# The last image's first two quarters: GpSimd additions against accumulating DMAs

## Chip, cores and metric

One core of a Trainium2 chip runs the whole program. The metric is the device time of one execution in microseconds. A time is given as the median of several runs; beside it stands one profiled execution, whose rows are quoted.

## The reference, cut to what matters

```python
# x: (16, 128, 64, 64) float32, NCHW
x = x + L0(gn(x))     # 3x3 convolution with three weight planes, each quantised, clipped and summed
x = x + L1(gn(x))     # attention-free layer on 128 channels, below
# gn: group norm, 32 groups of 4 channels

def L1(x):            # xf = x as (b, 128, 4096)
    q, k, v = Wq @ xf, Wk @ xf, Wv @ xf           # 64 x 4096 each
    ek = exp(k)
    num, den = exp(B) @ (ek * v), exp(B) @ ek
    return Wm @ (q * (num / den))                 # 128 x 4096
```

The change concerns the last "+": the sum of L1's output and its input x (the residual) for the last image.

## The kernel before

The channels lie on the 128 partitions. An image is 4096 pixels and goes in four quarters k = 0 to 3 of PX = 1024 columns (512 KB of float32 each). Four buffers `xr[0..3]` form a ring of images: an image is loaded into one, the first layer's result is added in place, then the second layer's result is added in place, and the quarters are stored from it. The phases are a software pipeline: while image p is in the first layer's convolution, p-1 and p-2 are in the second layer. The order of the work is written out by hand in slots of a phase, separately for each engine; semaphores tie the engines together.

In a normal image, a quarter of the second layer ends so: TensorE multiplies by Wm into PSUM (`mix`, L684), ScalarE copies the result from PSUM to the buffer `y2[k % 2]` (a part of `shared`) in `evict` (L964), GpSimd issues a DMA from `y2` onto `xr` with an addition on the way (`add_mix`, L1695), and its landing is counted by the semaphore `y_added[k % 2]`. SP waits for it (L438) and issues the store to DRAM (`store`, L440). GpSimd's own arithmetic in the body is the low halves of the split operands and the small statistics.

The last image runs behind the last convolution, with nothing beside it, in the order of the table LAST_ORDER (keys and values, sums, queries, mix, each with its quarter). Its four quarters end in two ways:

- Quarters 2 and 3: VectorE adds straight from PSUM to `xr` (`second_residual`, L1456) and raises `second_done`.
- Quarters 0 and 1: ScalarE copies from PSUM to `y2[k]` (`last_evict`, L973, raising `last_evicted`), and GpSimd adds `y2[k]` to `xr` in two halves of 512 columns (`last_add`, L1676 to L1681, raising `last_added` once per half). It is the last work in GpSimd's program.

SP stores the last image's quarters in the order 0, 1, 2, 3. Before each one it waits for that quarter's addition: `last_added` at 2 and 4, then `second_done` at 1 and 2 (L436). As a queue works in order, a wait for quarter 1 also holds back quarters 2 and 3. At the very end SP waits for all stores to land (L494). `y_added` counts 32 per image on each of its two semaphores, since each landing adds 16.

Of the kernel before, what the change touches and what calls it, by code (L numbers as in the profile page):

```python
# [20 lines left out]
ALU = mybir.AluOpType  # L21
# [6 lines left out]
B, H, W = 16, 64, 64  # L28
# [6 lines left out]
PX = ROWS * W  # L35
HALF = PX // 2
# [73 lines left out]
def conv_layers_kernel(nc, x, g_pos, g_neg, bias, in_factor, out_factor, Wq, Wk, Wv, Bm, Wm, out):  # L110
# [6 lines left out]
    with ctx:  # L117
        def sb(name, shape, dt=F32):
            return ctx.enter_context(nc.sbuf_tensor(name, shape, dt))

        def sem(name):
            return ctx.enter_context(nc.semaphore(name))
# [3 lines left out]
        xr = [sb(f"xr{i}", [P, H * W]) for i in range(RING)]  # L126
# [7 lines left out]
        y2 = [shared[:, k * PX:(k + 1) * PX] for k in range(2)]  # L134
# [217 lines left out]
        y_added = [sem("y_added0"), sem("y_added1")]  # L352
        second_done = sem("second_done")
        last_evicted = sem("last_evicted")
        last_added = sem("last_added")

        def waits_apart(eng, *waits):

            values = [v if isinstance(v, int) else eng.to_reg(v) for _, v in waits]
            eng.wait_ge(consts_made, 1)
            for (s, _), v in zip(waits, values):
                eng.wait_ge(s, v)
# [27 lines left out]
        def nth(image, per_image, m, back=0):  # L392

            return image * per_image + (m + 1 - back * per_image)
# [22 lines left out]
        def phases(eng, phase):  # L417

            phase(0, 0, (False, False, True, True))
            phase(1, 1, (False, True, True, True))  # L420
            for p in range(2, B - 1):
                phase(p, p % RING, (True, True, True, True))
            phase(B - 1, (B - 1) % RING, (True, True, True, False))
            phase(B, B % RING, (True, True, False, False))

        @block.sync
        def _(sp):
            def load(image, m, g):
                cols = slice(g * PX, (g + 1) * PX)
                sp.dma_start(xr[m][:, cols].rearrange("p (a n) -> p a n", a=1),  # L430
                             x_v[:, bass.ds(image, 1), cols]).then_inc(loaded[g], 16)

            def store(image, m, k):

                if isinstance(image, int) and image == B - 1:
                    sp.wait_ge(*((last_added, 2 * k + 2) if k < 2 else (second_done, k - 1)))  # L436
                else:
                    sp.wait_ge(y_added[k % 2], nth(image, 32, 16 * (k // 2) + 15))  # L438
                cols = slice(k * PX, (k + 1) * PX)
                sp.dma_start(out_v[:, bass.ds(image, 1), cols],  # L440
                             xr[m][:, cols].rearrange("p (a n) -> p a n", a=1)
                             ).then_inc(stored[k], 16)

            for g in range(NG):
                load(0, 0, g)
            for t, src in ((gp, gp_v), (gn, gn_v)):
                sp.dma_start(t[:, 0:CK], src[:, 0, :]).then_inc(g_loaded[0], 16)
            sp.dma_start(inf[:, :], in_factor.partition_broadcast(P)).then_inc(factors_loaded, 16)
            for i in range(1, NP):
                sp.dma_start(gp[:, i * CK:(i + 1) * CK], gp_v[:, i, :]).then_inc(g_loaded[i], 16)  # L450
                sp.dma_start(gn[:, i * CK:(i + 1) * CK], gn_v[:, i, :]).then_inc(g_loaded[i], 16)
            sp.dma_start(bcol[:, :], bias.rearrange("(c a) -> c a", a=1)).then_inc(others_loaded, 16)
            sp.dma_start(outf[:, :], out_factor.partition_broadcast(P)).then_inc(others_loaded, 16)
            sp.dma_start(wqk_in[0:IC, :], Wq).then_inc(small_loaded, 16)
            sp.dma_start(wqk_in[IC:P, :], Wk).then_inc(small_loaded, 16)
            sp.dma_start(wv_in[0:IC, :], Wv).then_inc(small_loaded, 16)
            sp.wait_ge(zeroed, 1)
            sp.dma_start(bm_in[0:IC, 0:IC], Bm).then_inc(small_loaded, 16)
            sp.dma_start(bm_in[IC:P, IC:P], Bm).then_inc(small_loaded, 16)
            sp.dma_start(wm_in[:, 0:IC], Wm).then_inc(small_loaded, 16)  # L460
            sp.dma_start(wm_in[:, IC:P], Wm).then_inc(small_loaded, 16)
            sp.wait_ge(head_stats, NG)
            for g in range(NG):
                sp.wait_ge(stats_in[0], g + 1)
                load(1, 1, g)

            def phase(p, m, images):
                prev2, prev, cur, nxt = images
                if prev2:
                    for k in range(1, NG):  # L470
                        store(p - 2, (m + 2) % RING, k)
                if isinstance(p, int) and p == 0:

                    sp.wait_ge(w_turned, 9)
                    sp.wait_ge(sums_made, 2 * NP)
                if isinstance(p, int) and p == 1:
                    for i in range(NP):
                        sp.wait_ge(w_diff[i], 1)
                    sp.wait_ge(small_turned, 1)
                if nxt and not (isinstance(p, int) and p + 2 >= B):  # L480
                    for g in range(NG):
                        sp.wait_ge(stats_in[0], nth(p + 1, NG, g))
                        if prev2:
                            sp.wait_ge(stored[g], nth(p, 16, 15, 2))
                        load(p + 2, (m + 2) % RING, g)
                if prev and cur:
                    store(p - 1, (m + 3) % RING, 0)
                if not cur:
                    for k in range(NG):
                        store(p - 1, (m + 3) % RING, k)  # L490

            phases(sp, phase)
            for k in range(NG):
                sp.wait_ge(stored[k], 16 * B)  # L494
# [1091 lines left out]
        def _(pool):  # L1586
# [88 lines left out]

            def last_add(m, k):  # L1676

                for h in range(2):
                    waits_apart(pool, (last_evicted, k + 1))
                    xh = xr[m][:, k * PX + h * HALF:k * PX + (h + 1) * HALF]  # L1680
                    nc.gpsimd.tensor_tensor(xh, xh, y2[k][:, h * HALF:(h + 1) * HALF], ALU.add  # L1681
                                            ).then_inc(last_added, 1)

            def rows_low(image, parity, g):
                for k, pair in enumerate(PAIRS):
# [21 lines left out]
            def phase(p, m, images):  # L1707
                prev2, prev, cur, nxt = images
                before, two_before = (m + 3) % RING, (m + 2) % RING
                spread_at, moments_at, low_at = ((EACH if prev else FIRST)[name]  # L1710
                                                 for name in ("X_SPREAD", "X_MOMENTS", "LOW"))
                for slot in range(SLOTS):
                    second_layer(p, m, slot, images)
                    if nxt and slot == spread_at:
                        spread_stats(0, p + 1)
                    if prev and slot == X1_SPREAD:
                        spread_stats(1, p - 1)
                    if cur and slot in low_at[2:]:
                        rows_low(p, m % 2, low_at.index(slot))
                    if nxt and slot in low_at[:2]:  # L1720
                        rows_low(p + 1, 1 - m % 2, low_at.index(slot))
                    if nxt and slot == moments_at:
                        scale_x(p + 1)
                    if prev and slot == X1_MOMENTS:
                        scale_z(p - 1)
                if not cur:
                    add_mix(p - 2, two_before, 3)
                    last_rest(p - 1, 2, duo_flat[:, 0:PX])
                    last_rest(p - 1, 3, z32)
                    for k in range(2):  # L1730
                        last_add(before, k)
# [31 lines left out]
```

## Time and profile before

| | us |
|---|---|
| median of 3 runs | 1474.59 (1474.12 to 1475.69) |
| profiled execution, own time | 1475.87 |
| its span | 1473.8 |
| mean granted TensorE clock | 0.992 |
| TensorE busy | 1430.0 (97%) |
| VectorE busy | 1346.0 (91%) |
| ScalarE busy | 1194.6 (81%) |
| GpSimd busy | 555.5 (38%) |

The span goes from the first instruction of the program to the last; some 2 us of the execution lie around it. Engines in rows: PE is TensorE (PEld its weight loads), DVE is VectorE, ACT ScalarE, POOL GpSimd, SP SyncE; a q behind a name is that engine's queue, which issues DMAs. L440 is line 440 of the kernel. A row's tiles are written "out<-in", with buffer numbers left out, so that `xr<-shared` is any of the transfers from `y2` onto an image. A DMA's "us to landing" runs from the start of its issue until its semaphore has its full count.

### The profile page before, as it was taken

Reading aid. Unit: us, or ns where it says so; the run is one execution under the profiler, and the core shown is the slowest. Engines: PE = TensorE matmul, PEld = TensorE weight load, DVE = VectorE, ACT = ScalarE, POOL = GpSimd, SP = SyncE. Lnnn points to the kernel's source line nnn. Section 1 sums busy time; section 2 is a strip of 40 time slices with the busy share of each in tenths; the row PEclk is TensorE's granted clock in tenths of the full one; section 3 lists DMA queues with packets and bytes.
Section 4 is the critical chain, followed back from the end, with each engine's and each line's share of the span. In section 5 each row is a group of like instructions: output and inputs, shape, how many; then the busy total and the mean of one; then the engine's idle time right before and its main releaser. Section 6 shows DMA issues by size and latency. Waiting matters only on the chain. (4 is left out here: it accounts for less than half of the span.)

```text
span 1473.8 us, 24096 instructions
## 1 busy us (share of the span) xinstructions
PE 1430.0 (97%) x8632; PEld 664.1 (45%) x8632; DVE 1346.0 (91%) x2018; ACT 1194.6 (81%) x1569; POOL 555.5 (38%) x687
## 2 busy tenths in 40 slices
PE   3999999999999999999999999999999999999996
PEld 3644444444444444444444444444444444444442
DVE  7699898999999999998999999899999989999887
ACT  6658798887988888888887989788898888976674
POOL 2212335343433624334352433535244253433323
PEclk9999999999999999999999999999999999999998
DMA  5011012223222222412322231232322222222133
GB/s 216 7 52 58 1 30 58 90 56 114 58 53 91 58 87 58 115 44 57 101 58 86 58 115 33 55 101 58 101 58 71 73 58 86 58 58 58 30 79 122
DMA packets 29174, 103.85 MB, mean 70 GB/s; under 512 B 4032, under 2 KB 4224, under 8 KB 29056
## 3 DMA queue, kind: packets, MB, share of 16 engines
q1 hardware_dynamic: 20416, 70.86, 13.1%
q0 software_dynamic: 8640, 31.46, 11.3%
q8 instruction: 69, 1.13, 0.3%
q14 instruction: 49, 0.40, 0.1%
HBM read 37.29 MB, written 33.55 MB: 48 GB/s over the span
## 5 line engine op out<-in xcount | busy, mean ns | idle before, releaser
L537 PE MATMUL A<-T,WH 128*128 128x504 f16 (+1 forms) x1152 | 438.5, 381 | 1.2 <-ACT uall L892 0.5
L539 PE MATMUL A<-T,WL 128*128 128x504 f16 (+1 forms) x1152 | 437.3, 380 | 0.0
L538 PE MATMUL A<-T,WH 128*128 128x504 f16 (+1 forms) x1152 | 437.3, 380 | 0.0
L1689 POOL TENSOR_TENSOR T<-t,T 128x512 f16<-128x512 f32 x189 | 245.2, 1327 | 307.7 <-ACT T L813 307.7
L1665 POOL TENSOR_TENSOR zl<-z,zh 128x512 f16<-128x512 f32 x120 | 149.0, 1259 | 363.1 <-ACT zh L940 363.1
L855 ACT ACTIVATE junk<-xr,shift 128x1024 f16<-128x1024 f32 x244 | 280.2, 1148 | 6.9 <-DVE xr L1334 1.2
L537 PE MATMUL B<-T,WH 128*128 128x504 f16 (+1 forms) x576 | 219.7, 381 | 9.4 <-DVE T L1265 7.0
L538 PE MATMUL B<-T,WH 128*128 128x504 f16 (+1 forms) x576 | 220.0, 382 | 0.0
L539 PE MATMUL B<-T,WL 128*128 128x504 f16 (+1 forms) x576 | 219.9, 382 | 0.0
L537 PEld LDWEIGHTS A<-T,WH 128*128 128x128 f16 x1152 | 115.3, 100 | 172.6 <-issue 47.0
L539 PEld LDWEIGHTS A<-T,WL 128*128 128x128 f16 x1152 | 112.7, 98 | 136.2
L538 PEld LDWEIGHTS A<-T,WH 128*128 128x128 f16 x1152 | 112.7, 98 | 116.2
L892 ACT CAST uall<-A 128x1024 int16<-128x1024 f32 x96 | 96.2, 1002 | 43.9 <-PE A L539 43.9
L793 ACT ACTIVATE q<-xr,bi,sc 128x1024 int16<-128x1024 f32 x64 | 79.1, 1239 | 45.7 <-DVE f L1198 22.9
L884 ACT COPY m<-B 128x1024 f32<-128x1024 f32 x96 | 96.0, 1000 | 23.7 <-PE B L539 23.7
L813 ACT CAST T<-t 128x512 f16<-128x512 f32 x192 | 106.0, 615 | 6.8 <-DVE t L1230 3.9
L1695 POOL DMA_DIRECT2D xr<-shared x60 | 54.8, 914 | 99.7 <-ACT shared L964 99.7
L537 PEld LDWEIGHTS B<-T,WH 128*128 128x128 f16 x576 | 56.7, 98 | 78.8 <-issue 9.0
L1198 DVE SCALAR_TENSOR_TENSOR f<-f,q 128x1024 f32<-128x1024 f32 x64 | 90.4, 1414 | 1.5 <-ACT f L803 1.5
L964 ACT ACTIVATE shared<-B 128x1024 f32<-128x1024 f32 x60 | 61.4, 1023 | 34.1 <-PE B L684 32.9
L539 PEld LDWEIGHTS B<-T,WL 128*128 128x128 f16 x576 | 56.6, 98 | 68.7 <-issue 1.1
L538 PEld LDWEIGHTS B<-T,WH 128*128 128x128 f16 x576 | 56.6, 98 | 68.3 <-issue 1.1
(211 smaller groups left out, 2564.8 us busy)
## 6 DMA issues: line engine op xcount, KB each, us to landing
xr<-in_x_dram SPq DMA_DIRECT2D x64, 512.0 KB, 6.2
out_dram<-xr SPq DMA_DIRECT2D x64, 512.0 KB, 2.7
xr<-shared POOLq DMA_DIRECT2D x60, 512.0 KB, 4.6
xr<-in_L_conv_g_pos_dram SPq DMA_DIRECT2D x3, 576.0 KB, 10.0
xr<-in_L_conv_g_neg_dram SPq DMA_DIRECT2D x3, 576.0 KB, 11.5
xr<-in_L_conv_Wm_dram SPq DMA_DIRECT2D x2, 32.0 KB, 9.3
xr<-in_L_conv_Wq_dram SPq DMA_DIRECT2D x1, 32.0 KB, 11.1
xr<-in_L_conv_Wk_dram SPq DMA_DIRECT2D x1, 32.0 KB, 10.9
```

Of the source, the lines that this page charges most:

```text
L537: nc.tensor.matmul(to, wh, th, start=fresh and y == 1, stop=False, skip_group_check=True)
L538: nc.tensor.matmul(to, wh, tl, start=False, stop=False, skip_group_check=True)
L539: done = nc.tensor.matmul(to, wl, th, start=False, stop=y == 2, skip_group_check=True)
L793: nc.scalar.activation(q16[b][:, :], xr[m][:, q * PX:(q + 1) * PX], ACT.Identity, bias=bi1[:, :], scale=sc1[:, :]).then_inc(leveled, 1)
L813: nc.scalar.copy(T[:, 0, pair, g * TILES:(g + 1) * TILES, :, :], t32[:, pair]).then_inc(th_ready, 1)
L855: nc.scalar.activation(junk[:, :], src[:, q * PX:(q + 1) * PX], func, bias=shift[which][:, :], accum_out=moments[which][:, k, q:q + 1]).th ...
L884: nc.scalar.copy(m2[:, :, :], low_pair[:, :, :]).then_inc(m2_copied, 1)
L892: nc.scalar.copy(u[i].rearrange("p (t k c) -> p k t c", k=4, c=W)[:, 0:4:3], A[n % 2][:, :, :].rearrange("p e (t w) -> p e t w", w=W)).the ...
L964: nc.scalar.activation(y2[k % 2].rearrange("p (r c n) -> p c r n", r=2, n=QUART), low_pair[:, :, :].rearrange("p c (r n) -> p c r n", r=2) ...
L1198: nc.vector.scalar_tensor_tensor(out=f_rows(q), in0=f_rows(q), scalar=KAPPA, in1=integers(q), op0=ALU.add, op1=ALU.mult).then_inc(f_ready, 1)
L1665: nc.gpsimd.tensor_tensor(zl[0][:, cols], z32[:, cols], zh[0][:, cols], ALU.subtract).then_inc(zl_ready, 1)
L1689: nc.gpsimd.tensor_tensor(low, t32[:, pair, :, :, :].rearrange("p t e w -> p (t e w)"), high, ALU.subtract).then_inc(tl_ready, 1)
```

## The change

For the last image's quarters 0 and 1 GpSimd no longer adds. It waits for the eviction once and issues one accumulating DMA per quarter, of the form used for all other images, from `y2[k]` onto the quarter in `xr`, counted by `y_added[k]`. SP's waits for these two quarters change from `last_added` to `y_added[k]`: fifteen images have brought it to 32 * 15, and this landing adds 16. The semaphore `last_added` goes. Quarters 2 and 3 and all other images stay as they are.

```diff
-        last_added = sem("last_added")
...
             def store(image, m, k):
 
                 if isinstance(image, int) and image == B - 1:
-                    sp.wait_ge(*((last_added, 2 * k + 2) if k < 2 else (second_done, k - 1)))
+                    sp.wait_ge(*((y_added[k], 32 * (B - 1) + 16) if k < 2 else (second_done, k - 1)))
                 else:
                     sp.wait_ge(y_added[k % 2], nth(image, 32, 16 * (k // 2) + 15))
...
             def last_add(m, k):
 
-                for h in range(2):
-                    waits_apart(pool, (last_evicted, k + 1))
-                    xh = xr[m][:, k * PX + h * HALF:k * PX + (h + 1) * HALF]
-                    nc.gpsimd.tensor_tensor(xh, xh, y2[k][:, h * HALF:(h + 1) * HALF], ALU.add
-                                            ).then_inc(last_added, 1)
+                waits_apart(pool, (last_evicted, k + 1))
+                nc.gpsimd.dma_start(xr[m][:, k * PX:(k + 1) * PX], y2[k], accum_op=ALU.add
+                                    ).then_inc(y_added[k], 16)
```

## Rows read from the trace of the kernel before

**Rows 1.** The page, busy us (share of the span) and instructions of each engine:

```profile
PE 1430.0 (97%) x8632; PEld 664.1 (45%) x8632; DVE 1346.0 (91%) x2018; ACT 1194.6 (81%) x1569; POOL 555.5 (38%) x687
```

**Rows 2.** Chain that ended last, its end: start us, us, what:

```profile
1464.85 0.70 DVE f L1442
1465.55 0.04 issue
1465.60 0.84 PE B L629 x6
1466.43 1.07 PE A L684 x16
1467.50 0.02 issue
1467.53 1.29 DVE xr L1456 x2
1468.81 0.60 DVEq L117
1469.41 0.60 DVE xr L1456
```

**Rows 3.** SP's waits, 1440 to 1475: us in total, times, longest:

```profile
SPq L440 <- POOL xr L1681: 13.8, 2, 10.1
SPq L440 <- DVE xr L1456: 1.2, 2, 0.8
```

**Rows 4.** Timeline, ScalarE's evictions: start, us, line, tiles [idle before <-releaser]:

```profile
1460.31 1.02 ACT L973 ACTIVATE shared<-L 128x1024 f32<-128x1024 f32 x1 [0.45 <-PE L L684]
1464.45 1.02 ACT L973 ACTIVATE shared<-A 128x1024 f32<-128x1024 f32 x1 [1.09 <-PE A L684]
```

**Rows 5.** Timeline, GpSimd's last work, two instructions in each row:

```profile
1461.47 2.51 POOL L1681 TENSOR_TENSOR xr<-xr,shared 128x512 f32<-128x512 f32 x2 [4.59 <-ACT shared L973]
1465.62 2.51 POOL L1681 TENSOR_TENSOR xr<-xr,shared 128x512 f32<-128x512 f32 x2 [1.64 <-ACT shared L973]
```

**Rows 6.** The last image's stores issued by SP, then landing of k = 0, 1, 3:

```profile
1464.00 0.33 SPq L440 DMA_DIRECT2D out_dram<-xr  x1
1468.15 0.33 SPq L440 DMA_DIRECT2D out_dram<-xr  x1
1468.84 0.33 SPq L440 DMA_DIRECT2D out_dram<-xr  x1
1470.04 0.33 SPq L440 DMA_DIRECT2D out_dram<-xr  x1
...
out_dram<-xr SPq DMA_DIRECT2D x1, 512.0 KB, 2.6
out_dram<-xr SPq DMA_DIRECT2D x1, 512.0 KB, 2.7
out_dram<-xr SPq DMA_DIRECT2D x1, 512.0 KB, 3.3
```

**Rows 7.** Busy time by stretch; last three columns clock, DMA share, GB/s:

```profile
core 0: us, PE busy (x) PEld busy (x) DVE busy (x) ACT busy (x) POOL busy (x), PEclk, DMA share, GB/s
1306.30:1307.70 1.40, 1.40 (x8) 0.64 (x7) 1.40 (x3) 0.69 (x2) 0.88 (x1) 1.00 0.00 0
1307.70:1310.50 2.80, 2.80 (x15) 1.27 (x13) 2.70 (x3) 2.61 (x3) 0.00 (x0) 1.00 0.99 187
1464.10:1464.80 0.70, 0.70 (x14) 0.26 (x6) 0.68 (x1) 0.35 (x1) 0.00 (x0) 1.00 0.00 0
1464.80:1466.30 1.50, 1.05 (x10) 0.26 (x6) 1.30 (x3) 0.67 (x1) 0.68 (x1) 1.00 0.86 350
1468.20:1468.90 0.70, 0.12 (x4) 0.00 (x0) 0.70 (x3) 0.00 (x0) 0.00 (x0) 1.00 0.00 0
1468.90:1473.10 4.20, 0.00 (x0) 0.00 (x0) 1.11 (x2) 0.00 (x0) 0.00 (x0) 0.81 0.94 375
```

**Rows 8.** Line 1695, all accumulating DMAs: issue ns min/median/max, then landing:

```profile
L1695 POOL DMA_DIRECT2D xr<-shared x60: 827/918/1307, 205.7 to 1448.4; - x60
DMA to landing us min/median/max: 4.5/4.6/6.3
```

**Rows 9.** Timeline, two normal evictions and the accumulating DMAs behind them:

```profile
1304.65 1.02 ACT L964 ACTIVATE shared<-B 128x1024 f32<-128x1024 f32 x1 [1.54 <-PE B L684]
1306.22 0.95 POOL L1695 DMA_DIRECT2D xr<-shared  x1 [7.38 <-ACT shared L964]
1446.83 1.00 ACT L964 ACTIVATE shared<-B 128x1024 f32<-128x1024 f32 x1
1448.38 0.95 POOL L1695 DMA_DIRECT2D xr<-shared  x1 [3.86 <-ACT shared L964]
```

**Rows 10.** DMA queues: packets, MB, share, 1306.22 to 1311.22 and 1463.5 to 1467:

```profile
q0 software_dynamic: 144, 0.52, 55.3%
q1 hardware_dynamic: 144, 0.52, 37.0%
```

**Rows 11.** DMA queues, 641.4 to 647.4, slowest landing; last, 1461 to 1463:

```profile
641.44 0.83 POOL L1695 DMA_DIRECT2D xr<-shared  x1
q0 software_dynamic: 144, 0.52, 46.9%
q8 instruction: 1, 0.02, 1.0%
xr<-shared POOLq DMA_DIRECT2D x1, 512.0 KB, 6.3
...
DMA  0000000000000900000000000000000000000000
q8 instruction: 1, 0.02, 3.0%
```

**Rows 12.** Lines 1439 and 1442 (ns min/median/max), then timeline of VectorE's last:

```profile
L1439 DVE SCALAR_TENSOR_TENSOR f<-A,f x2: 692/692/692, 1458.0 to 1461.2; 128x512 f32<-128x512 f32 x2
L1442 DVE TENSOR_TENSOR f<-A,f x2: 691/692/692, 1458.7 to 1461.9; 128x512 f32<-128x512 f32 x2
...
1467.53 1.29 DVE L1456 SCALAR_TENSOR_TENSOR xr<-A,xr 128x512 f32<-128x512 f32 x2 [0.36 <-PE A L684]
1468.73 1.28 DVE L1456 SCALAR_TENSOR_TENSOR xr<-B,xr 128x512 f32<-128x512 f32 x2
```

## Prediction

> **What bounds the kernel now.** Three views in this order: the page for the whole, the chain of waits for the end, the queues' own timeline for what the chain leaves out. The page says that TensorE is busy for 97% of the span [rows 1], so the body is a matmul body and neither the DMA engines nor GpSimd (38%) can move it. The change touches only the last 12.3 us. There the chain of waits follows the second layer of the last image through TensorE, ScalarE and VectorE and ends with VectorE's residual additions at about 1470.0 [rows 2]. It ends there because the page's chain follows instructions. The span is 1473.8, so 3.8 us lie behind it, and those belong to the output stores. SP's view of waits names what it stood still for: 13.8 us in two waits for GpSimd's additions (L1681), only 1.2 us for VectorE's [rows 3]. SP works in order k = 0, 1, 2, 3, so its third and fourth store can't go before the second, whatever VectorE has done.
>
> How the end is composed: ScalarE's two evictions of L973 end at 1460.31 + 1.02 = 1461.33 and 1464.45 + 1.02 = 1465.47 [rows 4]. GpSimd starts 0.14 us behind each and adds for 2.51 us [rows 5], to 1463.98 and 1468.13; SP issues store 0 at 1464.00 and store 1 at 1468.15, then stores 2 and 3 at 1468.84 and 1470.04, 0.02 to 0.03 us behind VectorE's additions (1467.53 + 1.29 and 1468.73 + 1.28) [rows 2, 6, 12]. The DMA engines carry nothing from 1468.2 to 1468.9 and are then 0.94 busy for 4.2 us, 3.95 us of work for three stores [rows 7]. So the last three stores run back to back behind store 1, and the end is the issue of store 1 plus 5.65 us (1473.8 - 1468.15). VectorE, 1.9 us later than GpSimd, hides nothing: its stores queue behind GpSimd's.
>
> **What the change removes.** Four additions of 1.27 us on GpSimd (L1681, 5.0 us in all). They lie beside TensorE and VectorE, whose work doesn't wait for them; only SP does. Might VectorE's instructions get shorter without them? L1439 and L1442 take 692 ns under GpSimd's additions (1461.22, 1461.95) as without them (1457.98, 1458.70), minimum and maximum the same [rows 12]. I take 0. Nothing else waits for these additions.
>
> **What it adds.** Two accumulating DMAs of 512 KB from GpSimd, and SP waits for their landing. The trace has sixty of the same form (L1695), so their price is measured. (a) From the end of the eviction to the issue: 1304.65 + 1.02 = 1305.67 to 1306.22, and 1446.83 + 1.00 = 1447.83 to 1448.38: 0.55 us both times, where a GpSimd addition needs 0.14 [rows 4, 5, 9]. (b) From issue to landing: 4.5 / 4.6 / 6.3 us, minimum, median, maximum [rows 8]. I take 4.6. (c) The landing to SP's store: 0.02, as behind the additions. Where GpSimd's addition put 2.68 us (0.14 + 2.51 + 0.03) between eviction and store, the DMA puts 0.55 + 4.6 + 0.02 = 5.17: 2.5 us more. GpSimd has nothing queued behind; the first DMA's 0.95 us of issuing are over long before the second eviction ends.
>
> Store 0: 1461.33 + 5.17 = 1466.50 instead of 1464.00. It isn't the end. Store 1 without any disturbance: 1465.47 + 5.17 = 1470.64 instead of 1468.15, +2.5 us. Stores 2 and 3 have their data at 1468.82 and 1470.01 and now both stand behind SP's wait for the landing, so all three go in one burst as before, and the 5.65 us behind store 1 are unchanged. What hid before, VectorE's additions beside store 1, can't get any of the loss back.
>
> **What it moves: store 0 into the second accumulation.** Before, store 0's transfer (1464.8 to 1466.3) had the DMA engines alone [rows 7]. Now it is issued at 1466.50, its data move from 0.8 us later, 1467.3, and need 37.0% of 3.5 us, 1.3 us of all 16 engines [rows 7, 10]. The second accumulation is issued at 1465.47 + 0.55 = 1466.02 and its data move 1.5 us later, from 1467.5: in rows 7 an accumulation issued at 1306.22 has a share of 0.00 up to 1307.70 and then 0.99 for 2.8 us. So an accumulation has no gap into which a store would fit: its own 55.3% of 5 us are 2.77 us of all 16 engines [rows 10]. At 1467.5 the store has 1.3 - 0.2 = 1.1 us left. If the engines share their time without loss, the accumulation ends 1.1 us later whatever the order, and so do its landing and store 1: 1471.7.
>
> None of the 60 accumulations overlaps a store or a load, so this 1.1 is bounded by neighbours. Below: 0, if the two don't disturb each other (the sixty alone, 4.6). Above: the slowest one. It is issued at 641.44 and lands after 6.3; in its stretch the only foreign transfer is one instruction fetch, 1.0% of 16 engines over 6.0 us, or 0.96 us on one engine [rows 11]. It cost 1.7 to 1.8 us, 1.8 times its own duration. By that ratio the 1.3 us of the store cost 2.3. I take 1.1, since saturation (0.99) is the row nearest to it.
>
> The Trainium skill ("DMA: Bandwidth & Descriptors", section "Issuing engines are not separate DMA queues") says that DMAs of all engines run on the same 16 DMA engines and interleave; no row of the trace of before shows it for these two kinds, and by it the shared case above is the one to expect. The same page ("Anatomy of one DMA — SWDGE (gpsimd) path") fits a DMA from GpSimd as 2.0 us plus bytes over 436 GB/s, which is 3.2 us for 512 KB; the rows differ, 4.5 at least. By that figure, worked out here as an estimate, store 1 would be only 1.1 us later and the time about 1475.7; it is a milder form of the first rival below, and the sixty landings decide against it.
>
> **Sum.** 2.5 + 1.1 = 3.6 us. The profiled execution took 1475.87 us with a span of 1473.8; the same tail gives 1479.5 with a span of 1477.4. The median of the runs is 1474.59, 1.3 us below the profiled one, so the forecast is 1474.59 + 3.6 = 1478.2 us, 0.24% slower. About 0.2%, 2.95 us, is what a measurement can tell from no change; that is 1477.5.
>
> **The rivals.**
> (1) Not slower: a quick landing. If an accumulation landed within 2.1 us of its issue (1468.13 - 1466.02), store 1 would go no later than now. Nothing in the profile speaks for it: the quickest of sixty took 4.5 us, and 2.77 us of data alone exceed 2.1. Even then little is won, for store 3 can't be issued before 1470.04, and alone it lands in 2.6 instead of 3.3 us [rows 6]: 1474.6 for a landing of 2.1 us, at best 1473.9. 2%. (The Trainium skill's figure of 3.2 us, cited above, would put this rival at 1475.7.)
> (2) The two transfers don't disturb each other (other parts of the engines, or store 0 late enough to miss): +2.5 us, 1477.1, within 0.2%. For it: the accumulation reads two operands for each write, so the engines might hide a store under it. Against it: the share of 0.99. 20%.
> (3) The collision costs more than its work, as behind the fetch of rows 11, or a fetch joins it: +2.5 + 2.3 = 4.8, 1479.4. One fetch runs at about 1461.7 [rows 11], just ahead of the first accumulation; if that lands later by up to 1.7 us, store 0 follows later too and still overlaps the second one. 13%.
> (4) The tail does any of this and the body shifts beside it: GpSimd's program is a few instructions shorter, and its fetches and those of the others fall elsewhere. The runs of before differ by 1.6 us (1474.12 to 1475.69), which is about its size: 1476.5 to 1479.5. 5%.
>
> **How the numbers follow.** The forecast, shared without loss, has 60%: 1478.2, its own range 1477.5 to 1478.9 from the spread of a median. Slower by over 0.2% (above 1477.5): 0.93 of these 60, all of the 13, a seventh of the 20, two of the 5: 74%. Faster by over 0.2% would need 2.95 us out of a tail that holds 0.7 at most (rival 1): 2%, from the shift. Within 0.2%: 24%. The range goes from rival 2 less 0.3 for the spread, 1476.8, to rival 3 plus 0.4, 1479.8.
>
> **What would show it.** GpSimd's issues at about 1461.9 and 1466.0, no L1681; landings 4.6 and about 5.7 us later; SP's wait for store 1 put down to the DMA, issue at about 1471.7, stores 2 and 3 within a microsecond behind it; the DMA engines busy from 1467.3 to about 1471.4, a gap of some 1.1 us, then 4.1 us of stores; the chain up to 1470.0 unchanged. The forecast is wrong if the second landing stays at 4.6 (rival 2), if it exceeds 6.3 (rival 3), or if the eviction at 1465.47 has moved, since then the body or the chain has.

## The result

| | us |
|---|---|
| before, median of 16 runs | 1475.18 (1474.02 to 1476.0) |
| after, median of 16 runs | 1477.9 (1476.83 to 1478.79) |
| ratio after / before | 1.0017, 95% interval 1.0010 to 1.0024 |
| span of the profiled execution, before | 1473.8 |
| span of the profiled execution, after | 1476.3 |

Two executions on record, one of the kernel before (5972 us) and the profiled one of the run with only quarter 0 by DMA (8470 us), took several times as long as all others and are in no ratio here.

The change costs 2.5 us by the spans and 2.7 us by the medians, about 0.17%. The forecast was 1478.2 us and +3.6 us. The time was nearer than the step: over 16 runs the kernel before has a median of 1475.18, not the 1474.59 from which the forecast started, and this 0.6 us hides part of a loss that was sized 0.9 to 1.1 us too high.

How to compare single profiles here: the moment at which ScalarE's second eviction (y2[1]) ends varies by 1.5 us from one profiled kernel to the next (1464.1 to 1465.6), which is the body. So each tail below is counted from that moment to the end of the span. Before, it is 1473.8 - 1465.47 = 8.3 us [rows 4]. After, 1464.41 + 1.02 = 1465.43, and 1476.3 - 1465.43 = 10.9 us.

After, the page's busy line, SP's waits from 1440 on, and ScalarE's and GpSimd's last rows of the timeline (start us, us, what):

```profile
PE 1429.6 (97%) x8632; PEld 663.7 (45%) x8632; DVE 1346.1 (91%) x2018; ACT 1194.6 (81%) x1569; POOL 552.1 (37%) x685
...
SPq L439 <- DMA xr<-shared: 33.5, 4, 13.2
...
1460.27 1.02 ACT L972 ACTIVATE shared<-L 128x1024 f32<-128x1024 f32 x1 [0.45 <-PE L L683]
1464.41 1.02 ACT L972 ACTIVATE shared<-A 128x1024 f32<-128x1024 f32 x1 [1.09 <-PE A L683]
...
1462.58 0.90 POOL L1678 DMA_DIRECT2D xr<-shared  x1 [5.74 <-issue]
1465.98 0.88 POOL L1678 DMA_DIRECT2D xr<-shared  x1 [2.50 <-ACT shared L972]
```

The body and the chain up to the evictions are those of rows 1 and 4. SP no longer waits for GpSimd's additions or for VectorE at all, only for landings: rows 3 had 1.2 us for VectorE. The second DMA is issued 0.55 us behind its eviction, as forecast. The first is issued at 1462.58, 1.29 us behind it, and the gap is put down to "issue", to nothing that the profile shows.

After, SP's four stores of the last image, k = 0 to 3 (timeline), each with its time to landing behind the four of them, then the two accumulations' times to landing:

```profile
1467.17 0.33 SPq L439 DMA_DIRECT2D out_dram<-xr  x1
1470.54 0.33 SPq L439 DMA_DIRECT2D out_dram<-xr  x1
1470.92 0.45 SPq L439 DMA_DIRECT2D out_dram<-xr  x1
1471.42 0.79 SPq L439 DMA_DIRECT2D out_dram<-xr  x1
...
out_dram<-xr SPq DMA_DIRECT2D x1, 512.0 KB, 4.7
out_dram<-xr SPq DMA_DIRECT2D x1, 512.0 KB, 2.7
out_dram<-xr SPq DMA_DIRECT2D x1, 512.0 KB, 3.7
out_dram<-xr SPq DMA_DIRECT2D x1, 512.0 KB, 4.4
...
xr<-shared POOLq DMA_DIRECT2D x1, 512.0 KB, 4.6
xr<-shared POOLq DMA_DIRECT2D x1, 512.0 KB, 4.5
```

Both accumulations land as if alone, after 4.6 and 4.5 us. The prediction had named exactly this ("the second landing stays at 4.6") as a sign that its forecast is wrong. It is store 0 that pays: 4.7 us to landing, where alone it took 2.6 [rows 6]. The DMA queues say which of the two was moving (share of the 16 engines; 1467.3 to 1470.0, then 1470.3 to 1475.5):

```profile
q0 software_dynamic: 128, 0.52, 101.7%
...
q1 hardware_dynamic: 547, 1.98, 95.9%
```

Between 1467.3 and 1470.0 there is no packet of a store, although store 0 was issued at 1467.17 and would have moved from 1468.0 (0.8 us behind its issue, as in rows 6 and 7). So the two did meet, but not in the way forecast: the accumulation was there first and went through whole, and the store waited. From 1470.0 four stores run back to back, without the gap of some 1.1 us that the forecast had ahead of the last three.

### The profile page after: what moved, and what is told of

Its sections match the earlier page's. It is cut to its first block and busy times, and to the rows that moved or that the text cites. A ratio compares the mean times of both kernels' runs of the same rounds, so it can differ in the third digit from the quotient of the medians.

```text
span 1476.3 us, 24092 instructions
## 1 busy us (share of the span) xinstructions
PE 1429.6 (97%) x8632; PEld 663.7 (45%) x8632; DVE 1346.1 (91%) x2018; ACT 1194.6 (81%) x1569; POOL 552.1 (37%) x685
## 3 DMA queue, kind: packets, MB, share of 16 engines
q0 software_dynamic: 8928, 32.51, 11.6%
## 6 DMA issues: line engine op xcount, KB each, us to landing
xr<-in_L_conv_g_pos_dram SPq DMA_DIRECT2D x3, 576.0 KB, 10.2
```

## The experiments

In all of them the tail is the end of the span less the end of the second eviction; 8.3 us before, 10.9 after.

### One quarter at a time

GpSimd adds quarter 0 as before, and only quarter 1 goes by DMA (SP's wait for quarter 1 changes to `y_added[1]`, as in the change; not shown):

```diff
 def last_add(m, k):
+    if k == 1:
+        waits_apart(pool, (last_evicted, k + 1))
+        nc.gpsimd.dma_start(xr[m][:, k * PX:(k + 1) * PX], y2[k], accum_op=ALU.add).then_inc(y_added[k], 16)
+        return
     for h in range(2):
...
```

> Quarter 0 is added by GpSimd as before, quarter 1 by the DMA. Store 0 is then issued near 1464.0 and its data (1464.8 to 1466.2) are through before the second accumulation starts (about 1467.5), so nothing meets it. Theory A (the landing of the second accumulation sets the end, the wait of store 0 in the changed kernel costs nothing of its own): store 1 goes at about 1470.5, the span ends at 1476.2, the same as the changed kernel, +2.4 us on the kernel before. Theory B (the end of the changed kernel is the backlog of four stores from 1470.0): with one store less in it the three others end near 1475.0 or less, the span at 1475.2 or less, +1.4 us or less.

Measured: median 1477.97 us of 10 runs, ratio 1.0019 (1.0009 to 1.0029), so this half of the change carries the loss. Timeline (second eviction, DMA, store 1), then the landing:

```profile
1463.73 1.02 ACT L973 ACTIVATE shared<-A 128x1024 f32<-128x1024 f32 x1 [1.09 <-PE A L684]
1466.04 0.90 POOL L1680 DMA_DIRECT2D xr<-shared  x1 [2.79 <-issue]
1470.61 0.33 SPq L440 DMA_DIRECT2D out_dram<-xr  x1
...
xr<-shared POOLq DMA_DIRECT2D x1, 512.0 KB, 4.6
```

Store 0 was long out of the way, yet from the issue of store 1 to the end there are 1476.3 - 1470.61 = 5.7 us, as in the changed kernel (1476.3 - 1470.54 = 5.8) and before (5.65). The backlog alone, theory B, would have given about 1.3 us less, the work of one store (3.95 us for three in rows 7). The tail is 11.6, not the 10.9 expected, since here the late issue (1466.04, 1.29 us behind the eviction's end at 1464.75) falls on the quarter that counts. This run alone doesn't settle which theory holds in the changed kernel; the runs on SP's order below do.

The mirror image, only quarter 0 by DMA (the same edit with k == 0):

> Quarter 0 is added by the DMA, quarter 1 by GpSimd. Theory A: the first accumulation lands near 1466.5 to 1467.2, no second one is there, store 0 moves its data at once (0.8 us behind its issue) and store 1 goes at 1468.15 as before; four stores run back to back from about 1468.0, end of the data 1473.3, span about 1474.1, +0.2 to +0.4 us on the kernel before. If the DMA for quarter 0 carries a cost of its own at the end (its late issue, 1.3 us behind the eviction in the changed kernel, or a delay of GpSimd's additions behind it), the span ends at 1475 or later. If store 0 is slow to start here too (data more than 1.5 us behind its issue), it was not the second accumulation that held it back in the changed kernel.

Measured: ratio 1.0005 (0.9995 to 1.0014), no difference that can be told. Its tail was read from the same kernel, profiled again:

> The kernel with the DMA for quarter 0 and GpSimd's additions for quarter 1, once more, for a profile of it. The first accumulation is issued 1.29 us behind the eviction and lands 4.6 us later, store 0's data start 0.8 us behind its issue, GpSimd's additions start 0.14 us behind the second eviction, store 1 is issued 2.7 us behind that eviction, and the span ends 8.4 to 8.8 us behind it, against 8.3 in the kernel before and 10.9 in the changed one.

```profile
1461.59 0.90 POOL L1680 DMA_DIRECT2D xr<-shared  x1 [5.61 <-issue]
1464.60 2.50 POOL L1686 TENSOR_TENSOR xr<-xr,shared 128x512 f32<-128x512 f32 x2 [2.11 <-ACT shared L973]
...
1466.19 0.33 SPq L440 DMA_DIRECT2D out_dram<-xr  x1
1467.12 0.33 SPq L440 DMA_DIRECT2D out_dram<-xr  x1
...
out_dram<-xr SPq DMA_DIRECT2D x1, 512.0 KB, 2.7
```

Store 0 follows a landing of 4.6 us and takes its usual 2.7, for no accumulation is beside it. The span ends at 1473.2, 8.8 us behind the eviction (1463.42 + 1.02): quarter 0 by DMA costs 0.4 us of tail, by this one profile.

### Who goes first, and why

If the store was held up only because the accumulation's data had started before its own, a store that starts first should hold up the accumulation. Quarter 1 by DMA, store 0 kept back by one more wait:

```diff
+                if isinstance(image, int) and image == B - 1 and k == 0:
+                    sp.wait_ge(o_ready, NG * (B - 1) + 3)
                 cols = slice(k * PX, (k + 1) * PX)
```

> As the run with the DMA for quarter 1 alone, but SP holds store 0 back until VectorE has gated quarter 2 (about 1466.1), so that its data start near 1466.9, half a microsecond ahead of the second accumulation's at 1467.45. Theory C (each DMA engine drains the packets that one queue has given it before it turns to the other): the store goes first and is through by about 1468.3; the accumulation starts behind it and lands about 0.8 us later than alone, 5.3 to 5.5 us behind its issue. Theory D (shared packet by packet without loss): the same landing of 5.3 to 5.6, but the store's data last until after 1469. Theory E (the accumulation goes first whatever was there): it lands after 4.5 to 4.6 and the store's data stop at 1467.5 and end after 1470.2. The span follows the landing: 1477.0 in C and D, 1476.2 in E.

Measured: inconclusive for the most part. The accumulation was late by its 0.74 us again (issued at 1466.72, the store at 1466.18) and met only the end of the store; it landed after 4.8 us, the store after 2.7, span 1477.3. The landing expected was 5.3 to 5.5. So the store was kept back longer (`o_ready` at `NG * B`):

> As the run with the DMA for quarter 1 alone, but SP holds store 0 back until VectorE has gated quarter 3 (1467.1), so that its data start at about 1467.9 and the second accumulation's would start at about 1468.2, in the middle of the store. Theory C (a DMA engine finishes what one queue has given it before it takes the other's): the store's data are through by 1469.3, the accumulation's start there, and it lands 5.7 us behind its issue instead of 4.6; span 1478.1. Theory D (shared packet by packet): the same landing, but the store's data last until after 1470.3. Theory E (the accumulation always goes first, which the changed kernel alone allows too): landing 4.6 and the store's data end after 1470.9; span 1477.0.

Measured: the accumulation issued at 1466.55 landed after 5.7 us, the store issued at 1467.03 after 3.3, span 1478.0, tail 12.7. Queues from 1467.8 to 1469.1, share of the 16 engines:

```profile
q1 hardware_dynamic: 117, 0.48, 91.9%
q0 software_dynamic: 7, 0.03, 11.8%
```

The accumulation would have moved from 1468.0 (1466.55 + 1.5); up to 1469.1 it has 7 of its 144 packets through, the store 117. The store was issued later, but its data came first (1467.8). That is what theory C expects: what comes first is finished first. Theory E is refuted by the 5.7, theory D by the queues. The change of turns isn't clean: up to 1469.7 the store has 136 of its 144 packets through, and of its 16 smallest (under 512 B) 8 are missing. So some engines turned before the store's last small packets, and it lands after 3.3 us instead of 2.7.

The Trainium skill ("DMA: Bandwidth & Descriptors", section "Queues, rings and completion order") says that an engine takes the queues in turn and drains a whole packet of some 9 to 17 descriptors of one before it switches. Here each DMA is 144 of the profile's packets on 16 engines, 9 on each if they are spread evenly. If each of these is one descriptor of the page, which no row shows, one such turn is one whole DMA. The order of service in the runs agrees with it (117 packets against 7), but for the store's last small ones.

### The late first issue

> The changed kernel with 24 additional waits on a semaphore that was satisfied long ago, in GpSimd's program ahead of its last operand splits, which moves its last instructions by 24 places. In the changed kernel the first accumulation is issued 1.29 us behind the eviction instead of 0.55, ending with an instruction fetch (1461.7 to 1462.7). If GpSimd waited for that fetch of its own program, the fetch now comes earlier, the first issue goes back to 0.55 us behind the eviction (about 1461.9) and the fetch at 1461.7 is gone. If it was the first DMA of its kind behind a pause or another engine's fetch, the issue stays at 1.29. The end stays where it is in both, since the second accumulation sets it: span 1476.2.

The edit is a loop of 24 `pool.wait_ge(consts_made, 1)` ahead of `last_rest(p - 1, 2, ...)`. Measured: first eviction 1459.60 + 1.03, issue at 1461.91, 1.28 us again, and the instruction fetch stays 0.4 us behind the eviction (1461.03, in the changed kernel 1461.71), so it doesn't come from the shifted part of GpSimd's program. The tail is 10.8, as expected. In the run with the DMA for quarter 1 alone the fetch is far away, and the delay of 1.29 us is there all the same. Its DMA queues from 1461.0 to 1461.5, 5 us ahead of the issue at 1466.04:

```profile
q8 instruction: 1, 0.02, 17.9%
```

So neither the fetch nor the exact place of the instructions explains it. Next, one more DMA, early (its tile `spare`, its semaphores and SP's wait for it at the very end are not shown):

```diff
+            def extra_add():
+                nc.gpsimd.memset(spare[:, :, :], 0.0).then_inc(spare_set, 1)
+                pool.wait_ge(spare_set, 1)
+                nc.gpsimd.dma_start(spare[:, 0, :], spare[:, 1, :], accum_op=ALU.add).then_inc(spare_moved, 16)
...
+                if not cur:
+                    extra_add()
```

> The changed kernel with one more small accumulating DMA (256 KB of zeros onto zeros, no one waits for it) in GpSimd's program some 80 us before the end. In all kernels so far the first DMA of the last image, the 61st of GpSimd's, is issued 1.25 us behind its wait and the one after it 0.5 us. If that delay belongs to the count, it moves to the one before (the last of image 14, 0.5 us so far) and the first of the last image has 0.5. If it belongs to the place in the program, it stays. The span stays 10.9 us behind the second eviction in both cases.

The edit moves 128 x 256 float32, so 128 KB and not 256, and GpSimd issues it at 1432.15, 44 us before the end. The reading doesn't hang on either: it comes ahead of the last two DMAs of image 14.

Timeline: image 14's last eviction and its DMA, now GpSimd's 61st; the last image's two DMAs and its second eviction; store 0. Then landings of store 0 and of the second accumulation, and the DMA queues from 1466.1 to 1467.2:

```profile
1446.29 1.00 ACT L967 ACTIVATE shared<-B 128x1024 f32<-128x1024 f32 x1
1448.57 0.97 POOL L1702 DMA_DIRECT2D xr<-shared  x1 [4.59 <-issue]
...
1460.51 0.89 POOL L1688 DMA_DIRECT2D xr<-shared  x1 [4.97 <-ACT shared L976]
1463.08 1.02 ACT L976 ACTIVATE shared<-A 128x1024 f32<-128x1024 f32 x1 [1.09 <-PE A L687]
1464.66 0.86 POOL L1688 DMA_DIRECT2D xr<-shared  x1 [3.26 <-ACT shared L976]
...
1465.06 0.33 SPq L442 DMA_DIRECT2D out_dram<-xr  x1
...
out_dram<-xr SPq DMA_DIRECT2D x1, 512.0 KB, 2.6
xr<-shared POOLq DMA_DIRECT2D x1, 512.0 KB, 5.6
...
q1 hardware_dynamic: 108, 0.43, 98.7%
q0 software_dynamic: 2, 0.01, 4.0%
```

The delay moved with the count: 1448.57 is 1.28 us behind its eviction (1447.29), where rows 9 have 0.55 for the DMA at this place, and the last image's first (1460.51) is 0.55 behind its own eviction (1459.96). What happens at the 61st DMA isn't known; only that it goes with the count, or with something that grows with it, and not with the place.

This run also is the forecast's own case, which the changed kernel missed by 0.7 us. With the first issue on time, store 0 goes out at 1465.06 and its data, 0.8 us behind the issue, start some 0.3 us ahead of where the accumulation's would (1464.66 + 1.5). Up to 1467.2 the accumulation has 2 packets through against the store's 108, and it is the accumulation that lands late: 5.6 us, +1.1. The tail is 1476.1 - 1464.10 = 12.0 us, 3.7 more than before; the forecast had 3.6. My own expectation, 10.9, was wrong: I took the two orders to cost the same.

### What sets the end: SP's order or the engines

SP's loop over the last image's stores runs over (0, 2, 3, 1) instead of 0, 1, 2, 3. First with quarter 1 alone by DMA, then in the changed kernel:

> As the run with the DMA for quarter 1 alone, but SP issues the last image's stores in the order 0, 2, 3, 1. Stores 2 and 3 then don't stand behind SP's wait for the accumulation, only behind the accumulation in the DMA engines: their data run from its end, store 1 joins the queue while they run, and the 1.2 us between the end of the accumulation's data and the first store's are filled. The span ends about 10.2 us behind the second eviction instead of 11.6. If SP's order costs nothing (the engines' share sets the end there too), it stays at 11.6.

> The changed kernel with the stores in the order 0, 2, 3, 1. There store 0 already waits in the engines for the end of the second accumulation and its 1.35 us fill the gap in which SP waits for the landing, so four stores are back to back in either order: the span ends 10.8 us behind the second eviction, as in the changed kernel. If the landing were what sets its end, the reordering would bring it to 9.5.

| by DMA | SP's order | issue of 2nd accumulation | end of span | difference |
|---|---|---|---|---|
| quarters 0, 1 (the change) | 0 1 2 3 | 1465.98 | 1476.3 | 10.3 |
| quarters 0, 1 | 0 2 3 1 | 1465.38 | 1475.6 | 10.2 |
| quarter 1 | 0 1 2 3 | 1466.04 | 1476.3 | 10.3 |
| quarter 1 | 0 2 3 1 | 1466.07 | 1475.0 | 8.9 |

Busy time by stretch (the column before the last is the share of the DMA engines): the changed kernel, then quarter 1 alone in the order 0 1 2 3, then quarter 1 alone in the order 0 2 3 1:

```profile
1470.00:1471.40 1.40, 0.00 (x0) 0.00 (x0) 0.00 (x0) 0.00 (x0) 0.00 (x0) 0.99 0.99 380
1471.40:1475.50 4.10, 0.00 (x0) 0.00 (x0) 0.00 (x0) 0.00 (x0) 0.00 (x0) 0.50 0.96 382
...
1470.30:1471.40 1.10, 0.00 (x0) 0.00 (x0) 0.00 (x0) 0.00 (x0) 0.00 (x0) 0.65 0.00 0
1471.40:1475.50 4.10, 0.00 (x0) 0.00 (x0) 0.00 (x0) 0.00 (x0) 0.00 (x0) 0.50 0.96 384
...
1467.50:1470.10 2.60, 0.12 (x4) 0.00 (x0) 1.81 (x4) 0.00 (x0) 0.00 (x0) 1.00 1.05 202
1470.10:1474.20 4.10, 0.00 (x0) 0.00 (x0) 0.00 (x0) 0.00 (x0) 0.00 (x0) 0.57 0.97 384
```

The tails are 10.2 us (quarter 1 alone) and 10.8 us (the changed kernel), as expected in both cases. Two limits coincide in the changed kernel. Behind the accumulation's last data the landing and the next store's start take 1.1 to 1.4 us; with quarter 1 alone the engines idle there (share 0.00), in the changed kernel the delayed store 0 fills just this gap (0.99). Take only the backlog away, or only SP's order, and nothing is won. With both gone the tail is 1.3 us shorter, and the three stores follow the accumulation without a gap.

### The price by size, and the other way round

Of quarter 1 only the second half by DMA, the first half by GpSimd behind the issue:

> Quarter 0 added by GpSimd; of quarter 1 the second half (256 KB) by an accumulating DMA, the first half by GpSimd behind the issue of it. It measures the price by size. The whole quarter lands 4.6 us behind its issue, 2.77 of them data. If the rest, 1.8 us, is fixed, the half lands after 1.8 + 1.4 = 3.2 us; if the engines' time goes by the packets and not by bytes, after 4.6. It is the first such DMA of the last image, so its issue is expected 1.29 us behind the eviction. Store 1 then goes 4.5 us behind the eviction and the span ends 5.65 behind that, 10.2.

Issue and landing, and the DMA queues from 1468.0 to 1470.5:

```profile
1466.93 0.90 POOL L1682 DMA_DIRECT2D xr<-shared  x1 [2.77 <-issue]
xr<-shared POOLq DMA_DIRECT2D x1, 256.0 KB, 3.3
q0 software_dynamic: 144, 0.26, 61.1%
```

Measured: issue 1466.93 (1.29 behind the eviction), landing 3.3 us later, tail 10.4. With 4.6 for the whole, the second 256 KB cost 1.3 us, and a line through the two sizes leaves 2.0 us fixed. The half has as many packets as the whole, 144, and its data take 61.1% of 2.5 us, 1.5 us of all 16 engines against 2.77. So outside the data there are 1.8 us at both sizes, and the time goes mostly, not wholly, by bytes.

Last, the kernel before with each eviction in two halves, so that GpSimd starts earlier:

```diff
-                nc.scalar.activation(y2[k].rearrange("p (r c n) -> p c r n", r=2, n=QUART),
...
+                for h in range(2):
+                    nc.scalar.activation(y2[k][:, h * HALF:(h + 1) * HALF].rearrange("p (c n) -> p c n", n=QUART),
+                                         pair[:, :, h * QUART:(h + 1) * QUART], ACT.Identity,
+                                         scale=1.0 / WSCALE).then_inc(last_evicted, 1)
...
-                    waits_apart(pool, (last_evicted, k + 1))
+                    waits_apart(pool, (last_evicted, 2 * k + h + 1))
```

> The kernel before with each of ScalarE's two evictions of the last image split into two of 512 columns, so that GpSimd's first addition of a quarter starts behind the first half. The first addition should start 0.4 us earlier, the second directly behind it, and store 1 leave about 2.3 instead of 2.7 us behind the end of what was one eviction. The three last stores stay back to back, so the span ends about 7.9 instead of 8.3 us behind that point: 0.4 us, 0.03%, which only the profile can show, not the time. If SP's store or the store of quarter 3 sets the end instead, it stays at 8.3.

```profile
1464.27 1.08 ACT L974 ACTIVATE shared<-A 128x512 f32<-128x512 f32 x2 [1.09 <-PE A L684]
1465.01 2.50 POOL L1682 TENSOR_TENSOR xr<-xr,shared 128x512 f32<-128x512 f32 x2 [1.64 <-ACT shared L974]
1467.54 0.33 SPq L440 DMA_DIRECT2D out_dram<-xr  x1
```

GpSimd starts while ScalarE still copies the second half; store 1 leaves 2.25 us behind 1465.29, where one eviction would have ended, instead of 2.68, and the span of 1473.2 ends 7.9 behind it. The 0.4 us are there, but the ratio is 0.9999 (0.9989 to 1.0009): it beats the changed kernel, and the one before by nothing that a time can show.

## Why the prediction was right or wrong

**Right, by half: what sets the end.** The stores of the last image behind SP's in-order wait for the landing. The 5.65 us behind store 1's issue stayed 5.8, and the VectorE quarters hid nothing. But the gap ahead of the last three stores did not come: the delayed store 0 filled it, and with SP's order changed (0 2 3 1) the end stayed. The backlog in the DMA engines sets it just as much.

**Right: the price of the accumulation.** 0.55 + 4.6 + 0.02 for the second quarter, 5.1 measured (1470.54 - 1465.43). The term of 2.5 us is the whole loss: 10.9 - 8.3 = 2.5 with the profile's decimals.

**Right: removing GpSimd's additions gives VectorE nothing.** The chain ends alike. Its last row after the change starts 3.94 us behind the second eviction's end, as before (1469.41 - 1465.47 [rows 2, 4]):

```profile
1469.37 0.60 DVE xr L1455
```

**Wrong: the first issue.** The forecast took 0.55 us for both. The 61st DMA of GpSimd took 1.29. The trace of before could not show it: it has sixty.

**Wrong: store 0 in the second accumulation, +1.1 us.** The step said "the accumulation ends 1.1 us later whatever the order". That holds if the engines share, or if the store comes first. They don't share; the first takes all, and the interleaving that the prediction expected isn't seen between these two (128 packets against none). The term measured 0: the accumulation's landing stayed at 4.5. The 0.74 us of the late issue put the store second, so it waited, at a place where its wait was free. With the issue on time (the run with the extra DMA) the term is right to 0.1 us. So the size hangs on a race: the forecast had store 0's data 0.2 us ahead of the accumulation's (1467.3 against 1467.5), in the changed kernel they were due 0.5 us behind (1468.0 against 1467.5).

**Luck.** The measured 1477.9 us lies 0.3 us from the forecast of 1478.2. That is not the working's merit: the term of 1.1 us did not come, and the kernel before was 0.6 us slower over 16 runs than over the 3 from which the forecast started. And 1478.2 was forecast as the shared case, at 60%, a mechanism that the runs refute.

**Rival 2** named the right size, +2.5 us, for the wrong reason: "the two transfers don't disturb each other". They did; store 0 took 4.7 us for 2.6. **Rival 3** fell: where the two met, the cost was at most 1.1 us (5.7 and 5.6 instead of 4.6 and 4.5), not 2.3, and the fetch at 1461.71 didn't delay the first landing (4.6). **Rival 1** fell: no landing came near 2.1 us; even 256 KB took 3.3. **Rival 4**, a shift of the body, isn't seen in the profiles compared: the second eviction ends at 1465.43 instead of 1465.47.

**The size against 0.2%.** Slower by over 0.2% had 74%, within 0.2% had 24%; it is 0.17%, with an interval from 0.10 to 0.24. That it is slower is clear; on which side of 0.2% it lies isn't. The forecast had 0.24%, and the 0.07% between are 1.0 us, about the term that did not come.

## What to carry to other kernels

An accumulating DMA can be cheap in the body, where its 5 us lie behind other work (here TensorE is busy for 97% of the span with sixty of them in it; no run replaced those), and dear in a drain: compare eviction to landing (5.2 us) with eviction to the end of the addition (2.7 us), and count what SP's order holds back behind it. Where two transfers like these may meet, work out which one's data start first, for here that one was served first, nearly whole, and the other waited; a shift of 0.74 us upstream decided who paid. When two limits end at the same moment, an experiment that lifts one of them shows nothing: lift both before saying which binds.

## What the runs showed of the hardware

- GpSimd's 61st DMA was issued 1.28 to 1.29 us behind its eviction instead of 0.55 in each of the ten profiled kernels that have one, and the delay moved by one place when a DMA was added. In the kernel before, the 29th and 57th take longer to issue (1.31 and 1.29 us against a median of 0.92 [rows 8]) and land after 5.0 us. Cause open.
- Two DMAs of 512 KB from GpSimd and SP are not interleaved: in the changed kernel 128 packets of the accumulation and none of the store in 2.7 us, with the store first 108 of the store against 2 in 1.1 us.
- An accumulation from SBUF to SBUF took 3.3 us for 256 KB and 4.6 us for 512 KB. A line through these two gives 2.0 us fixed and 1.3 us for each 256 KB, about 200 GB/s, half of a store's 384. The Trainium skill ("DMA: Bandwidth & Descriptors", section "Anatomy of one DMA — SWDGE (gpsimd) path") gives 2.0 us and bytes over 436 GB/s for a DMA from GpSimd: the fixed part of this line agrees, the rate doesn't hold for the accumulations here.
- SP's issue takes 0.33 us, but 0.45 and 0.79 us for the third and fourth store in the changed kernel, issued within 0.5 us of the one before. The number of stores in flight doesn't explain it: with quarter 1 alone in the order 0 2 3 1 the last store is issued 1.3 us behind the one before, with two in flight, and takes 0.33 us. Cause open.
